# Blocks 2 to 5 of a four-layer residual chain: the adapter's output kept in feature rows and turned through DRAM

## The reference

```
x = x + L0(x)     # gated layer with causal scans and a layer norm
x = x + L1(x)     # x @ W[cat] + b
x = x + L2(x)     # adapter: see below
x = x + L3(x)     # x @ W[subject]^T + b

L2(x):  h      = relu(x @ W1 + b1)          # 512 -> 128
        z      = x + h @ W2 + b2            # 128 -> 512, plus the layer's own input
        normed = (z - mean(z)) * rsqrt(var(z) + 1e-5)
        return normed * gamma + beta
```

## Time and profile before

| | us |
|---|---|
| median of 3 runs | 721.21 (720.27 to 721.30) |
| the profiled execution | 721.11 |
| its span, first to last instruction | 719.3 |
| outside the span | 1.8 |
| TensorE busy, share of the span | 99% |
| VectorE | 76% |
| ScalarE | 52% |
| GpSimd | 20% |

### The profile page before, as it was taken

The page is one execution under the profiler, slowest core; times in us unless marked ns, Lnnn a source line. Parts: engine busy times, 40 slices in busy tenths (PEclk is TensorE's granted clock), DMA queues, the critical chain, the costliest instruction groups (busy, mean ns, idle before and its releaser), DMA issues.

```text
span 719.3 us, 10000 instructions
## 1 busy us (share of the span) xinstructions
PE 713.5 (99%) x3261; PEld 588.5 (82%) x3261; DVE 547.1 (76%) x824; ACT 372.2 (52%) x554; POOL 140.8 (20%) x256
## 2 busy tenths in 40 slices
PE   9999999999999999999999999999999999999998
PEld 8877888888888888888888888888888888888886
DVE  5799796695596587579569569987888887897583
ACT  4365446435535545544644553564756574664530
POOL 2000030022004004004003103313262242123210
PEclk9999999999999999999999999999999999999999
DMA  7959307934953970990891582657155658353312
GB/s 220 264 108 181 63 1 107 197 78 80 194 107 58 175 146 16 177 183 3 134 183 62 97 213 100 165 160 248 65 146 184 183 132 182 103 134 103 88 73 88
DMA packets 141871, 93.55 MB, mean 130 GB/s; under 512 B 108703, under 2 KB 124094, under 8 KB 140046
## 3 DMA queue, kind: packets, MB, share of 16 engines
q1 hardware_dynamic: 139310, 86.56, 52.8%
q10 hardware_dynamic: 1184, 4.23, 1.7%
q0 software_dynamic: 1344, 2.36, 1.3%
HBM read 32.28 MB, written 25.20 MB: 80 GB/s over the span
## 4 chain that ended last, share of the span: by engine, by line
PE 94%; DVE 4%; issue 1%; ACT 1%; POOL 0%; ACTq 0%; DVEq 0%; POOLq 0%
PE pc L728 12%; PE pc L730 12%; PE pc L729 12%; PE pt L728 8%; PE pt L730 8%; PE pt L729 8%; PE pm L728 4%; PE pm L730 4%; PE pm L729 4%; PE pm L854 4%; PE pm L856 4%; PE pm L855 4%; PE pm L735 3%; PE pm L980 1%; PE pm L978 1%; PE pm L979 1%
## 5 line engine op out<-in xcount | busy, mean ns | idle before, releaser
L728 PE MATMUL pc<-x_h,wg_h 128*128 128x512 f32 x224 | 87.7, 391 | 0.1
L730 PE MATMUL pc<-x_h,wg_l 128*128 128x512 f32 x224 | 87.3, 390 | 0.0
L729 PE MATMUL pc<-x_l,wg_h 128*128 128x512 f32 x224 | 87.3, 390 | 0.0
L1585 DVE TENSOR_TENSOR_SCAN stage_b<-alpha,carry,stage_b 128x512 f32<-128x512 f32 x64 | 78.5, 1269 | 0.0
L1226 ACT ACTIVATE ctx_t<-ctx_t,col_all 128x512 f32<-128x512 f32 x32 | 23.1, 723 | 54.3 <-DVE ctx_t L1565 54.3
L728 PEld LDWEIGHTS pc<-x_h,wg_h 128*128 128x128 f32 x224 | 42.1, 188 | 10.6 <-issue 1.9
L854 PE MATMUL pm<-t_h,wt_h 128*128 128x512 f32 x128 | 50.1, 392 | 0.6 <-DVE t_l L1598 0.6
L855 PE MATMUL pm<-t_l,wt_h 128*128 128x512 f32 x128 | 49.9, 390 | 0.0
L856 PE MATMUL pm<-t_h,wt_l 128*128 128x512 f32 x128 | 49.9, 389 | 0.0
L730 PE MATMUL pm<-wo_h,s_l 128*128 128x512 f32 x128 | 49.8, 389 | 0.0
L728 PE MATMUL pm<-wo_h,s_h 128*128 128x512 f32 x128 | 49.8, 389 | 0.0
(11 more groups left out here) (264 smaller groups left out, 1952.7 us busy)
## 6 DMA issues: line engine op xcount, KB each, us to landing
x_planes<-x_pairs SPq DMA_DIRECT2D x56, 256.0 KB, 7.0
xt_scratch<-x_t SPq DMA_DIRECT2D x8, 1024.0 KB, 10.0
n_scratch<-stage_a SPq DMA_DIRECT2D x8, 1024.0 KB, 9.6
ctx_t<-xt_scratch SPq DMA_DIRECT2D x16, 512.0 KB, 6.2
out_dram<-x_tok SPq DMA_DIRECT2D x28, 256.0 KB, 2.3
x_pairs<-n_scratch SPq DMA_DIRECT2D x10, 512.0 KB, 5.3
mod<-mod_scratch ACTq DMA_DIRECT2D x8, 512.0 KB, 3.7
x_planes<-stage_b SPq DMA_DIRECT2D x60, 64.0 KB, 2.3
```

Source lines behind the costliest of these rows:

```text
L728: nc.tensor.matmul(acc, ah, bh, start=start and q == 0, stop=False)
L729: nc.tensor.matmul(acc, ah, bl, start=False, stop=False)
L730: last = nc.tensor.matmul(acc, al, bh, start=False, stop=stop and q == n - 1)
L1585: nc.vector.tensor_tensor_scan(tr[:, m % 2, :], alpha[:, 1 + d:2 + d].to_broadcast([P, BLK]), tr[:, m % 2, :], carry[:, D - d, m:m + 1], A ...
```

## The change

In blocks 2 to 5 (`by_feature(i)`: `FIRST_F = 2` up to `BY_TOKEN = 6`):

- TensorE leaves the L1 product of chunk m in its PSUM bank, in feature rows, and `zz_product(i, b, m)` adds the second adapter product to it there with three matmuls. Each block uses four open banks in place of two (`pc[0], pc[1], pt[0], pt[1]` for block 2, `pm[0..3]` for blocks 3 to 5). The 16 transposes of a block in `xx_product` are gone.
- ScalarE evicts each bank a third time (`z_evict`) into `stage_a` and issues one DMA of 256 KB for it to `z_scratch` in DRAM.
- SyncE's `load_z(i)` waits until all four have landed and loads the block back into `stage_a` with four DMAs, in pieces of 128 bytes, so that every 32x32 square stands at its place. It is the first thing in the queue's round i+1.
- VectorE turns the squares in place (`z_turn`, four per block) and takes the statistics from `stage_a`, both now in step i+1.
- The norm of block i is then taken from `stage_a` into `x_planes`. ScalarE scales the squares of block i at the head of step i+2 and no more at the end of step i+1, and VectorE adds them (`x3_sum_part`) there too.
- ScalarE and VectorE get an order of their own for steps 3 to 6 (`middle_step2`), with the norm's first tile ahead of the relu.

The core of the diff:

```diff
+        def by_feature(i):
+            return FIRST_F <= i < BY_TOKEN
 ...
+            def load_z(i):
+                sp.wait_ge(z_out, (z_before(i) + NC) * 16)
+                exchanged = z_scratch[bass.ds(i, 1)].rearrange("z m p t -> (z m p t)").rearrange(
+                    "(b i k q f) -> q i k b f", i=32, k=TILES, q=4, f=32)
+                for q in range(4):
+                    sp.dma_start(stage_a[32 * q:32 * q + 32, :, :].rearrange("i k (b f) -> i k b f", f=32),
+                                 exchanged[q]).then_inc(z_in, 16)
 ...
             for i in range(2, NBLK):
+                if by_feature(i - 1):
+                    load_z(i - 1)
                 if i == PER_SEQ:
                     load_l3_half(1)
                 move_n2(i - 1)
 ...
+            def zz_product(i, b, m):
+                if m == 0:
+                    pe.wait_ge(hid_hi, i + 1)
+                    pe.wait_ge(hid_lo, i + 1)
+                bank = l1_bank(i, m)[:, :]
+                wh, wl = (w[:, out_cols(m)] for w in w2_w(b))
+                nc.tensor.matmul(bank, wh, h_h[:, :], start=False, stop=False, skip_group_check=True)
+                nc.tensor.matmul(bank, wh, h_l[:, :], start=False, stop=False, skip_group_check=True)
+                nc.tensor.matmul(bank, wl, h_h[:, :], start=False, stop=True,
+                                 skip_group_check=True).then_inc(xx_mm, 1)
 ...
# ScalarE
+            def z_evict(i):
+                if i == FIRST_F:
+                    act.wait_ge(n2_squares, (i - 1) * TILES)
+                else:
+                    act.wait_ge(n2_act, n2_acts(i - 1))
+                for m in range(NC + 1):
+                    if m < NC:
+                        act.wait_ge(xx_mm, i * TILES + m + 1)
+                        nc.scalar.activation(stage_a[:, m, :], l1_bank(i, m)[:, :], ACT.Identity,
+                                             bias=seq["b1b2"][:, i // PER_SEQ, m:m + 1]).then_inc(z_done, 1)
+                    if m > 0:
+                        act.wait_ge(z_done, z_before(i) + m)
+                        act.dma_start(z_scratch[bass.ds(i, 1)].rearrange("z m p t -> (z m) p t")[m - 1],
+                                      stage_a[:, m - 1, :]).then_inc(z_out, 16)
+            def middle_step2(i):
+                if i > 3:
+                    for m in range(NC):
+                        scale_n2(i - 2, m)
+                x2_parts(i, 0)
+                x3_hi_part(i - 2, 0)
+                x3_hi_part(i - 2, 1)
+                x2_parts(i, 1)
+                x3_hi_part(i - 2, 2)
+                x3_hi_part(i - 2, 3)
+                x2_parts(i, 2)
+                x2_parts(i, 3)
+                normalise(i - 1, 0)
+                relu_part(i)
+                normalise(i - 1, 1)
+                normalise(i - 1, 2)
+                normalise(i - 1, 3)
+                if i in (3, 5):
+                    subject_hi(1, (i - 3, i - 2))
+                for c in range(NC):
+                    y_hi_part(i + 1, c)
+                if by_feature(i):
+                    z_evict(i)
 ...
# VectorE
+            def z_turn(i, k):
+                if k == 0:
+                    dve.wait_ge(z_in, (z_before(i) + NC) * 16)
+                nc.vector.transpose(stage_a[:, k, :].rearrange("p (b i) -> p b i", i=32),
+                                    stage_a[:, k, :].rearrange("p (b f) -> p b f", f=32)).then_inc(z_turned, 1)
+            def middle_step2(i):
+                j = i - 2
+                if i > 3:
+                    x3_sum_part(j, 0)
+                    x3_sum_part(j, 1)
+                x2_lo_part(i, 0)
+                if i > 3:
+                    x3_sum_part(j, 2)
+                    x3_sum_part(j, 3)
+                x3_lo_part(j, 0)
+                x3_lo_part(j, 1)
+                x2_lo_part(i, 1)
+                x3_lo_part(j, 2)
+                x3_lo_part(j, 3)
+                z_turn(i - 1, 0)
+                norm2_stats(i - 1, 0)
+                x2_lo_part(i, 2)
+                for k in (1, 2):
+                    z_turn(i - 1, k)
+                    norm2_stats(i - 1, k)
+                x2_lo_part(i, 3)
+                z_turn(i - 1, 3)
+                norm2_stats(i - 1, 3)
+                output(j, 0)
+                for c in range(NC):
+                    turn_y(i + 1, (c,))
+                    y_sum_part(i + 1, c)
+                turn_squares(i - 1, 0)
+                hid_lo_part(i)
+                for k in range(1, TILES):
+                    turn_squares(i - 1, k)
+                output(j, 1)
 ...
+                for c in range(NC):
+                    y_lo_part(i + 1, c)
+                output(j, 2)
 ...
+                output(j, 3)
```

More of the change, by code:

```diff
@@ L998, in l3_tile @@
                     after(pe, out_ready, j * TILES + max(k - 1, 0))
+                if j == 0 and k >= 2:
+                    pe.wait_ge(n2_act, n2_acts(0) + (1 if k == 2 else 3))
+                if j == 1 and k == 0:
+                    pe.wait_ge(z_done, NC)
                 tok = out_cols(k)
@@ L1043, in second_step2 @@
                 l3_tile(0, 3)
-                for k in range(TILES):
-                    xx_product(2, 0, k)
+                for m in range(NC):
+                    zz_product(2, 0, m)
             def step2(i):
@@ L1057, in step2 @@
                 for k in range(TILES):
-                    xx_product(i, b, k)
+                    if by_feature(i):
+                        zz_product(i, b, k)
+                    else:
+                        xx_product(i, b, k)
                 l3_tile(i - 2, 3)
@@ L1428, in step2 @@
+            def step2(i):
+                if i > 2:
+                    for m in range(NC):
+                        scale_n2(i - 2, m)
+                    for m in range(NC):
+                        x3_hi_part(i - 2, m)
+                x2_parts(i, 0)
+                if i == 2:
+                    x2_parts(i, 1)
+                normalise(i - 1, 0)
+                if i > 2:
+                    x2_parts(i, 1)
                 normalise(i - 1, 1)
@@ L1470, in _ @@
             adapter_hi(1)
-            for i in range(2, NBLK):
-                step2(i)
+            step2(2)
+            for i in range(3, LAST):
+                middle_step2(i)
+            step2(LAST)
             for m in range(NC):
@@ L1862, in turn_squares @@
                     dve.wait_ge(x3_lo, j * NC)
[L1863 removed]
+                src = x_planes if by_feature(j) else stage_a
+                nc.vector.transpose(squares[:, :, k, :], src[:, k, :].rearrange("p (f i) -> p f i", i=32)
                                     ).then_inc(n2_squares, 1)
@@ L1869, in adapter_lo @@
                     nc.vector.tensor_tensor(wl, raw, f32(wh), ALU.subtract).then_inc(l2_lo, 1)
+            def middle_step2(i):
[30 more added lines that the diff above has]
+                output(j, 1)
+                if i == 4:
+                    subject_turn(1, (2, 3))
+                if i in (3, 5):
+                    subject_lo(1, (i - 3, i - 2))
+                for c in range(NC):
+                    y_lo_part(i + 1, c)
+                output(j, 2)
+                if not by_feature(i):
+                    for k in range(TILES):
+                        norm2_stats(i, k)
+                output(j, 3)
             def step2(i):
@@ L1926, in step2 @@
                     x3_lo_part(i - 1, 3)
-                for k in range(TILES):
-                    norm2_stats(i, k)
+                if not by_feature(i):
+                    for k in range(TILES):
+                        norm2_stats(i, k)
                 if i < LAST:
```

96 lines of the change are left out of this document (54 added, 42 removed).

## The result

The changed kernel takes 794.86 us (794.51 to 795.45, 4 runs) beside 721.25 us (720.27 to 724.58) for the kernel before: ratio 1.1005, with a 95% interval of 1.0976 to 1.1035. That is 10% slower. The profiled execution has a span of 793.6 us (before 719.3).

The account below looks back on a forecast made before the run. TensorE, busy 713.5 of 719.3 us, bounds the kernel. hid_lo(3) at 578.5, block-to-block loops of 40.3, 45.3 and 45.3, then 33.8 + 34.3 and 1.8 outside the span give 779 us, 8% slower; range 751 to 795.

Parts of the forecast that it names:

- All upper values together: Whole run with the start and both parts of each loop at their upper bounds: 790 us.
- the rival of TensorE's clock: Half clock after idling, at w1_product and two L3 tiles, delays zz_product 3.4 us in four steps: 793 us; chance 0.08.
- Leg two: From hid_lo(i) to z(i)'s landing, through ScalarE's and SyncE's queues: 25 us once, 30 twice; upper bounds 26.9 and 31.8.
- The end: From hid_lo(6) to the end of the span: 33.8 us to xx_product(7), then 34.3 unchanged, 68.1 us.
- TensorE's gain: Four transposes fewer per tile, 0.45 us each tile, 7.2 us over sixteen tiles of blocks 2 to 5.
- Where it starts: First trip, block 2: z(2) lands at 563.2 us and hid_lo(3) is at 578.5 us.
- Leg one: From z(i-1)'s landing to hid_lo(i), through turns, statistics, norm's scale, normalise and relu: 15.3 us, bounds 14.0 and 16.0.
- t + 17.5: Step 7: low half needed by l1_product(7, 2), 17.5 us after hid_lo(6) (called t) instead of 12.7.
- Edits costed at nothing: Third eviction and DMA issues on ScalarE (up to 1 us a loop if uncovered), and the other reordering: priced at zero.
- Hidden: z(i-1) lands within 9.7 us of the first L1 matmul in every step, so nothing waits: 713.9 us; chance 0.04.
- a delay once: Only the first trip costs some 10 us; later ones overlap with the longer steps: 725 us; chance 0.05.
- The write's landing decides: SyncE's queue costs nothing, z's write to DRAM sets loops of 35.0, 34 and 35 us: 752 us; chance 0.08.

Follow-up runs that it names:

- e1_z_first: The changed kernel with SyncE's load_z(i) moved into round i, behind two stores and ahead of load_y(i+2); 773.1 us.
- e5_spin: The changed kernel with extra transposes into free banks (70 ahead of w1_product in steps 3 to 6, 80 ahead of l1_product(7, 2)) to keep TensorE busy; 796.5 us.
- e6_store_first: The changed kernel with SyncE's store_out(i-2, 0) ahead of move_n2(i-1) instead of behind it; 792.3 us.
- e13_order_store_first: The kernel before, with its own way of z but the change's new engine order, plus store_out(i-2, 0) ahead of move_n2(i-1); 734.3 us.
- e8_order_only: The kernel before, with its own way of z, but scale_n2 and x3_sum at the head of the next step and the change's engine orders; 747.5 us.
- e7_no_trip_no_move: The changed kernel without z's trip through DRAM and without move_n2, so both exchanges of squares are left out; 731.0 us.
- e11_turns_first: The changed kernel without z's trip through DRAM, with VectorE's z_turn and statistics moved to the head of the step; 754.5 us.
- e12_turns_store_first: The changed kernel without z's DRAM trip, with VectorE's turns and statistics at the step's head and store_out(i-2, 0) ahead of move_n2(i-1); 749.6 us.
- e2_no_trip: The changed kernel without z's trip through DRAM: ScalarE's four DMAs and SyncE's load_z left out, z_turn waits for the eviction; 751.7 us.
- e3_long_rows: The changed kernel with load_z reading the same bytes in 2 KB rows instead of 128-byte pieces, squares not at their places; 793.2 us.
- e10_no_move: The changed kernel with z's trip kept but move_n2's DMAs left out, scale_n2 waiting for turn_squares alone; 767.2 us.

## Why the prediction was right or wrong, point by point

The sign, the mechanism and the place were right, and the time lies inside the range (751 to 795), though barely: 794.9 instead of 779. That it lies inside is luck. All upper values together gave only 790. The range reached 795 to make room for the rival of TensorE's clock (793), whose cause the runs refute. Leg two came out above its upper bound in all three loops. The end was forecast 6.8 us too short and had no bounds at all: it stands with the same value in the low sum and in the high one.

**What bounds the kernel, and TensorE's gain.** Right as read: 64 instructions less on TensorE, and nothing of it visible.

**Where it starts.** z(2) was forecast at 563.2 and turned at 563.8; hid_lo(3) was forecast at 578.5 and ended at 578.8.

**Leg one.** From z_turn to the end of hid_lo it is 14.95, 14.96, 15.65 and 15.66 us. The forecast was 15.3, from the earlier trace rows. A chain inside the engines could be added up from the rows to 0.4 us.

**Leg two** is where the loop went wrong. SyncE's timeline of the changed kernel, its round 3 and load_z(3) at the head of round 4, then load_z(4) and load_z(5):

```profile
580.97 8.22 SPq L334 DMA_DIRECT2D x_planes<-stage_b  x10
589.23 1.57 SPq L536 DMA_DIRECT2D out_dram<-x_tok  x2
590.89 0.89 SPq L503 DMA_DIRECT2D x_pairs<-n_scratch  x2
591.83 0.94 SPq L507 DMA_DIRECT2D ctx_t<-xt_scratch  x2
593.58 1.09 SPq L536 DMA_DIRECT2D out_dram<-x_tok  x2
594.72 9.73 SPq L531 DMA_DIRECT2D stage_a<-z_scratch  x4
...
642.92 8.70 SPq L531 DMA_DIRECT2D stage_a<-z_scratch  x4
...
689.65 10.03 SPq L531 DMA_DIRECT2D stage_a<-z_scratch  x4
```

The legs are 607.48 - 578.79 = 28.7, 32.0 and 33.0 us. I had 25, 30 and 30, and the bounds that I had called upper were 26.9 and 31.8. load_z begins 15.9, 20.5 and 19.5 us after hid_lo, not 12.4 and 18.6. The mis-sized term is move_n2, 6.2 us by the earlier trace rows and 8.2 to 8.8 now; with the stores and load_y behind it, load_z begins 3.5, 1.9 and 0.9 us later than forecast. The time from the first issue to the turn, 12.8, 11.6 and 13.4 us, is what the values chosen implied (25 - 12.4 = 12.6 and 30 - 18.6 = 11.4), except for the last. The three misses make 3.7 + 2.0 + 3.0, nearly 9 us of the 16. That SyncE's queue and not the write decides was right for this place of the load: e1_z_first moves it forward and wins 22 us.

**The end** is the other 6.8 us: 74.85 us from hid_lo(6), forecast 68.1. The changed kernel on VectorE, output(4, 2) of step 6 and the first x2_lo of step 7, then TensorE's first matmuls behind its wait, and their window:

```profile
730.33 0.69 DVE L1942 TENSOR_TENSOR x_tok<-pt,mod 128x512 f32<-128x512 f32 x1 [6.55 <-DMA out_dram<-x_tok]
...
740.03 0.74 DVE L1904 SCALAR_TENSOR_TENSOR s_l<-pc,seq_b,s_h 128x512 fp32r<-128x512 f32 x1
```

```profile
740.92 0.77 PE L759 MATMUL pc<-x_h,wo_h 128*128 128x512 f32 x1 [9.19 <-DVE s_l L1904]
741.48 0.63 PE L760 MATMUL pc<-x_l,wo_h 128*128 128x512 f32 x1
741.91 0.63 PE L761 MATMUL pc<-x_h,wo_l 128*128 128x512 f32 x1
```

```profile
736.00:745.00 9.00, 4.08 (x10) 3.25 (x11) 7.37 (x12) 6.85 (x11) 3.17 (x7) 0.50 0.08 29
```

I had followed scale_n2(5) through ScalarE and put l1_product(7, 2) at t + 17.5. It came at t + 22.2, since VectorE's statistics and x3 stood behind output(4, 2), and that behind a store that move_n2(5) had pushed back (store issued at 727.95). Its first ten matmuls then ran 0.43 us apart instead of 0.23, at a granted clock of 0.50, which costs 2 us. The tail of e5_spin, where the clock was kept up, is shorter by 2.4 us, which agrees. From xx_product(7) to the end nothing changed, 34.0 us against 34.3.

That the store is the cause is borne out by e6_store_first: its wait there is 2.0 us, and hid_lo(7) comes 33.5 us after hid_lo(6) instead of 37.5. Its tail is nevertheless only 0.7 us shorter. The timeline of e6_store_first shows what took the gain back:

```profile
744.26 3.00 POOL L334 DMA_DIRECT2D x_planes<-stage_b  x6 [13.24 <-DVE stage_b L1979]
...
747.28 0.33 SPq L536 DMA_DIRECT2D out_dram<-x_tok  x1
747.71 6.22 SPq L334 DMA_DIRECT2D x_planes<-stage_b  x10
...
756.30 2.81 DVE L1919 TENSOR_TENSOR stage_b<-stage_b,x_t 128x512 f32<-128x512 f32 x4 [3.61 <-ACT stage_b L1449]
```

GpSimd's share of move_n2(6) starts at 744.26. SyncE's starts 3.4 us later, since the store of block 5 that the edit put ahead of it has to wait for output(5, 0). So x3_sum(6) waits 3.6 us for scale_n2(6). The same 75 us of tail in e13_order_store_first carry this too (4.4 us of the same wait).

**Edits costed at nothing.** The third eviction and the DMA issues on ScalarE did no harm there, but probably slowed SyncE's issues (below). "The other reordering fills time in which VectorE waits" is the wrong sentence of the prediction. It is true only while z's trip is the longer loop. e8_order_only prices the reordering by itself at 26 us, more than three times what the change was to save. It did not spoil the number, because the longer loop hides it. It would have spoiled any advice drawn from the number: the fix of SyncE's queue was expected to bring 760 and brought 773.

**The rivals.** Hidden (713.9) and a delay once (725) are refuted by three loops that are all long. The write's landing decides (752): with z's load moved ahead of load_y (e1_z_first) 773 is reached, because the loop beneath takes over; the forecast of this rival lacked it too. TensorE's clock (793) names nearly the measured time, but not its cause. The clock does fall to 0.50 (1.2 of 2.4 GHz) after idle time, as the Trainium skill has it ("TensorE: Matmul & The Clock Gate", part 1), and this trace agrees; but in the changed kernel's loops the slow matmuls cost nothing, since the norm's scale comes later: e5_spin has them at full clock and its loops are no shorter. The price was to be 3.4 us in each of four steps and is about 2 us, once, in a step that I had not named.

**The rule weighed.** By the Trainium skill, "DMA: Bandwidth & Descriptors" (the fit in the section on the anatomy of one DMA), 1 MB would be an estimate of 4.4 us. The page fits one DMA issued by GpSimd; here SyncE issues four. Here it took 7.8 us in pieces with little else in flight (556.00 to 563.84), 6.6 us in long rows (557.04 to 563.60), and 11.6 to 13.4 us behind another load. The measurements decide: to go by the row of the same pattern was right, and behind load_y its 8.3 us were still too low.

**What stays open.** Where the last 2.5 us per loop of e7_no_trip_no_move come from (31.5 against a step of 29.0) was not separated; VectorE is the nearest candidate: in the loop shown it is busy for 28.6 us and its one long wait is 2.1 us, for x2 from ScalarE. What the fallen clock costs in e8_order_only, e11_turns_first and e12_turns_store_first is open too: only the changed kernel was also run with TensorE kept busy.

## What to carry to other kernels

Before work is moved by one step in a pipeline of in-order queues, walk every closed path from a product to the same product one block later, through each queue and each buffer that must come free, and compare each path's length with the step: the longest sets the time, and the next longest is what a repair will find. An exchange through DRAM is not priced by its bytes, but by what stands ahead of it in the issuing queue and by the data already in flight. And look for waits of 1 to 2 us in the old trace, such as a store that frees a buffer: each names a path with no room left.

## What the runs showed of the hardware

How long a DMA issue takes is not fixed by the engine and the DMA alone. move_n2's ten issues on SyncE take 6.2 to 6.3 us in rounds 3 to 5 of the kernel before and of e2_no_trip (up to 7.4 in rounds 6 and 7 of these two). In the changed kernel the same three rounds take 8.2 to 8.8 us, and in e3_long_rows, with short issues of z's load but the same writes of z on ScalarE, still 7.8 to 8.4. With the moves left out (e10_no_move) the load that follows is the slow one: its four issues take 8.4 us in round 4, where the changed kernel has 5.0, and e1_z_first 6.0. SyncE's timeline of e10_no_move, and of the changed kernel:

```profile
617.44 8.37 SPq L520 DMA_DIRECT2D x_pairs<-n_scratch  x4
```

```profile
634.63 5.03 SPq L520 DMA_DIRECT2D x_pairs<-n_scratch  x4
```

The slow issues are those beside ScalarE's four writes of z. In e10_no_move these are issued from 618.5 to 621.0, within the 8.37 us above. In the changed kernel they are issued from 626.9 to 630.0, within move_n2's ten (624.61 to 633.40), and over before the load at 634.63. That the writes slow SyncE's issues is inferred from these; no run delayed the writes alone.

Four loads of 256 KB in 128-byte pieces are issued in 4.8 us with little in flight and in 8.7 to 10.0 us behind load_y's data; in 2 KB rows they take 1.8 to 3.0 us. The sooner return of the queue did not bring z sooner by more than 2.4 us.
